# Routing beside attention: when the scatters of a token list are issued, and how its last tiles get in

## The reference

```python
x = x + xattn(layernorm(x), ctx, ctx)          # 16 heads of 32, projections with biases
h = layernorm(x).reshape(4096, 512)
logits = h @ router_weight.T + router_bias      # 8 experts
topk_vals, topk_idx = top_k(softmax(logits), 2)
gu = einsum('th,ehf->tef', h, gate_up_proj) + gate_up_bias
gate, up = minimum(gu[..., :I], 7), clip(gu[..., I:], -7, 7)
act = (up + 1) * gate * sigmoid(1.702 * gate)
down = einsum('tei,eih->teh', act, down_proj) + down_bias
x = x + einsum('teh,te->th', down, w)           # w: the two chosen weights of a token, else 0
```

## Time and profile before

| | us |
|---|---|
| timed runs, median of 3 (lowest to highest) | 1814.1 (1813.7 to 1815.97) |
| the profiled execution, its own time | 1809.48 |
| its span, from the first to the last instruction | 1807.8 |
| PE busy | 1630.6 (90%) |
| DVE busy | 1278.2 (71%) |
| ACT busy | 659.0 (36%) |
| POOL busy | 866.5 (48%) |
| mean granted TensorE clock | 0.956 |

### The profile page before, as it was taken

One profiled execution on the slowest core, in us unless ns is written; L12 is line 12 of the kernel. 1 busy time (PEld: TensorE's weight loads), 2 busy tenths in 40 slices (PEclk: granted clock), 3 DMA queues, 4 the chain that ended last, 5 costly groups with the idle time before them and its releaser, 6 DMA issues. The chain is left out here.

```text
span 1807.8 us, 30265 instructions
## 1 busy us (share of the span) xinstructions
PE 1630.6 (90%) x9591; PEld 1190.5 (66%) x9591; DVE 1278.2 (71%) x2424; ACT 659.0 (36%) x1273; POOL 866.5 (48%) x687
## 2 busy tenths in 40 slices
PE   5889999999989999999987319999999999999996
PEld 3555565555555555555543209999999998999995
DVE  4676777858768678686774537777888778767873
ACT  3344544435445344354442114223233224222320
POOL 4365565565665755656656331433334333333332
PEclk9999999989999999999998559999999999999998
DMA  6343343453363524333421261324343345333321
GB/s 214 84 117 75 97 116 90 117 64 101 113 89 91 114 77 131 74 110 77 89 65 30 54 188 40 104 83 164 137 170 117 90 147 176 89 94 131 122 77 64
DMA packets 101157, 188.94 MB, mean 105 GB/s; under 512 B 28531, under 2 KB 29683, under 8 KB 100992
## 3 DMA queue, kind: packets, MB, share of 16 engines
q1 hardware_dynamic: 79680, 124.16, 26.7%
q0 software_dynamic: 21312, 62.80, 11.1%
HBM read 204.23 MB, written 37.56 MB: 134 GB/s over the span
## 5 line engine op out<-in xcount | busy, mean ns | idle before, releaser
L763 DVE TENSOR_REDUCE negmax<-max_ps 128x2 f32<-128x1024 f32 x256 | 312.3, 1220 | 190.6 <-PE max_ps L520 156.8
L644 ACT ACTIVATE pt<-work 128x512 f32<-128x512 f32 x512 | 279.0, 594 | 263.8 <-PE work L532 237.0
L932 POOL TENSOR_TENSOR acc<-acc,pt 128x1024 f32<-128x1024 f32 x128 | 303.6, 2375 | 147.5 <-ACT pt L644 147.5
L1383 PE MATMUL gu_ps<-xgT_hi,wg_hi 128*128 128x256 f32 x1248 | 355.0, 284 | 0.0
L1383 PE MATMUL gu_ps<-xgT_hi,wg_lo 128*128 128x256 f32 x1248 | 351.8, 282 | 0.0
L1383 PE MATMUL gu_ps<-xgT_lo,wg_hi 128*128 128x256 f32 x1248 | 351.5, 282 | 0.0
L929 POOL TENSOR_TENSOR acc<-pt 128x1024 f32<-128x1024 f32 x64 | 153.2, 2394 | 215.3 <-PE work L552 148.8
L1383 PEld LDWEIGHTS gu_ps<-xgT_lo,wg_hi 128*128 128x128 f32 x1248 | 235.6, 189 | 0.1
L1383 PEld LDWEIGHTS gu_ps<-xgT_hi,wg_hi 128*128 128x128 f32 x1248 | 235.6, 189 | 0.1
L520 PE MATMUL max_ps<-ks,qs 96*128 96x512 f32 x512 | 203.8, 480 | 35.1 <-DVE negmax L763 19.8
L1383 PEld LDWEIGHTS gu_ps<-xgT_hi,wg_lo 128*128 128x128 f32 x1248 | 235.3, 189 | 0.0
(11 more groups left out here) (204 smaller groups left out, 2944.1 us busy)
## 6 DMA issues: line engine op xcount, KB each, us to landing
raw_g<-w_gate_up SPq DMA_DIRECT2D x39, 2048.0 KB
raw_d<-w_down SPq DMA_DIRECT2D x39, 1024.0 KB
ks<-k_hi SPq DMA_DIRECT2D x252, 64.0 KB
qs<-q_hi SPq DMA_DIRECT2D x252, 64.0 KB, 2.0
bd<-b_down SPq DMA_DIRECT2D x39, 256.0 KB
x_in<-x SPq DMA_DIRECT2D x32, 256.0 KB, 3.1
ctxT_raw<-ctx_t SPq DMA_DIRECT2D x32, 256.0 KB, 3.8
x<-x SPq DMA_DIRECT2D x32, 256.0 KB, 3.0
```

The lines of the kernel that those rows point to most:

```text
L644: e.activation(pt[k % 2][:, h, :], in_work("exp", u, k, h)[:, :], ACT.Exp, scale=scale).then_inc(exped.sem, 1)
L763: e.tensor_reduce(negmax[:, u % 2, n:n + 2], max_ps[:, :, :], AX.X, ALU.max, negate=True).then_inc(maxed.sem, 1)
L932: e.tensor_tensor(acc[:, heads, :], acc[:, heads, :], pt[k % 2][:, heads, :], ALU.add).then_inc(added.sem, 1)
L1383: ins = e.matmul(gu_ps[n % GU_BANKS][:, part, :], wg[s][pw][:, k, cols], xgT[s][px][:, k, :], start=(k == 0 and m == 0), stop=(k == KD - 1 ...
```

## The change

- `list` of groups 0 to 4: one tile a step, in round 3 of steps 4g + 11 to 4g + 14. Group 5: two tiles in rounds 2 and 3 of step 31, two in round 1 of step 32. Group 6: all three in round 4 of step 32. Groups 7 and 8, five tiles, are not scattered at all.
- The choice of experts of groups 0 to 5 stands in rounds 1, 2 and 3 of its step (`best` 0, `best` 1, and a new key `count`, which was the end of `best` 1), `soft` in round 5; `share` moves to round 1 of step 4g + 11.
- `place` of groups 7 and 8 only copies the ranks out of PSUM to `ranks`.
- In the routing stage POOL makes a row of 0 to 127 (`iota`); DVE computes for the last five tiles places in the padded order, splits them into a column (of 78) and a row (of 128), makes one-hot matrices `at_hot` (128 x 1280) and `col_hot` (128 x 780), multiplies the latter with the token numbers, and PE adds ten products of them into `list_ps`. The rest of the list is no longer gathered: SP loads all 256 rows of `token_list` with one DMA once the scatters are in, and two more matmuls with a matrix `choose` (built on DVE) pick the rows and add them into `list_ps`, in the place of the turn.
- `token_list` has 256 rows instead of 336; the indices by which the gather went, `slot_ended` to `row_i`, are gone.

```diff
-            for r, lag, *keys in ((2, 9, ("best", 0)), (3, 9, ("best", 1)), (4, 9, ("soft",)), (5, 9, ("share",)), (2, 10, ("rank",)), (3, 10, ("place",)),
-                                  (2, 11, ("list", 0), ("list", 1)), (3, 11, ("list", 2), ("list", 3))):
+            for r, lag, *keys in ((1, 9, ("best", 0)), (2, 9, ("best", 1)), (3, 9, ("count",)), (5, 9, ("soft",)),
+                                  (2, 10, ("rank",)), (3, 10, ("place",)), (1, 11, ("share",))):
...
+            g, t = divmod(s - 11, T)
+            if g in groups[:-4]:
+                at(3, ("list", g, t))
+            if s == units[-1]:
+                at(2, ("list", groups[-4], 0))
+                at(3, ("list", groups[-4], 1))
+            if s == units[-1] + 1:
+                at(1, ("list", groups[-4], 2), ("list", groups[-4], 3))
...
             if s == units[-1] + 1:
                 at(1, ("best", g, 0))
-                at(2, ("best", g, 1), ("soft", g), ("rank", g))
-                at(3, ("place", g))
-                at(4, ("share", g))
+                at(2, ("best", g, 1), ("count", g), ("rank", g))
+                at(3, ("place", g), ("soft", g))
+                at(4, ("share", g), *[("list", g, t) for t in range(GROUPS[g][1])])
             if s == units[-1] + 2:
-                at(0, *[("list", g, t) for t in range(GROUPS[g][1])])
                 g += 1
-                at(1, ("best", g, 0), ("best", g, 1), ("soft", g))
-                at(2, ("rank", g), ("place", g), *[("list", g, t) for t in range(GROUPS[g][1])])
-                at(3, ("best", g + 1, 0), ("best", g + 1, 1), ("soft", g + 1), ("rank", g + 1), ("share", g), ("place", g + 1), ("share", g + 1))
+                at(1, ("best", g, 0), ("best", g, 1), ("count", g))
+                at(2, ("rank", g), ("soft", g), ("place", g))
+                at(3, ("best", g + 1, 0), ("best", g + 1, 1), ("count", g + 1), ("soft", g + 1), ("rank", g + 1), ("share", g), ("place", g + 1), ("share", g + 1))
...
                 e.wait_ge(ranked.sem, ranked[g])
+                if g >= groups[-2]:
+                    e.tensor_copy(ranks[:, slots, :], in_work("rank", g)[:, 0:n * E].rearrange("p (t e) -> p t e", e=E)).then_inc(pos_made.sem, 1)
+                    return
...
+            e.wait_ge(consts_made, IOTA)
+            then(e.tensor_copy(iota[:, :], iota_i[:, :]))
             e.wait_ge(counted, 1)
...
+            then(e.tensor_tensor(ranks[:, late, :], ranks[:, late, :], start[:, :].unsqueeze(1).to_broadcast([P, left, E]), ALU.add))
+            last()
+            for s in range(TOP_K):
+                then(e.tensor_tensor(hot[s][:, late, :], hot[s][:, late, :], ranks[:, late, :], ALU.mult))
+            last()
+            for s in range(TOP_K):
+                then(e.tensor_reduce(pos_f[:, s, :], hot[s][:, late, :], AX.X, ALU.add))
+            last()
+            then(e.tensor_copy(pos_i[:, :, :], pos_f[:, :, :]))
+            last()
+            then(e.tensor_scalar(at_i[:, :, :], pos_i[:, :, :], P - 1, None, ALU.bitwise_and))
+            then(e.tensor_scalar(col_i[:, :, :], pos_i[:, :, :], SHIFT, None, ALU.arith_shift_right))
+            last()
+            then(e.tensor_copy(at_f[:, :, :], at_i[:, :, :]))
+            then(e.tensor_copy(col_f[:, :, :], col_i[:, :, :]))
+            last()
+            then(e.tensor_tensor(at_hot[:, :, :], iota[:, :].unsqueeze(1).to_broadcast([P, KT, P]),
+                                 at_f[:, :, :].rearrange("p s t -> p (s t)").unsqueeze(2).to_broadcast([P, KT, P]), ALU.is_equal))
+            flat_cols = col_hot[:, :, :, :].rearrange("p s t c -> p (s t) c")
+            then(e.tensor_tensor(flat_cols, iota[:, 0:SLOTS].unsqueeze(1).to_broadcast([P, KT, SLOTS]),
+                                 col_f[:, :, :].rearrange("p s t -> p (s t)").unsqueeze(2).to_broadcast([P, KT, SLOTS]), ALU.is_equal))
+            last()
+            for s in range(TOP_K):
+                then(e.tensor_tensor(col_hot[:, s, :, :], col_hot[:, s, :, :],
+                                     token[:, done_tiles:].unsqueeze(2).to_broadcast([P, left, SLOTS]), ALU.mult), ("late", s))
...
+            for c, number in enumerate((part, part_2)):
+                then(e.tensor_scalar(choose[:, c, :], row_slot[:, :], number[:, 0:1], None, ALU.is_equal), "choose")
...
-            e.wait_ge(columns_in, 16)
-            e.transpose(list_ps[:, :], columns[:, :], ident[0:SLOTS, 0:SLOTS]).then_inc(turned, 1)
+            for s in range(TOP_K):
+                e.wait_ge(vec, at["late", s])
+                for t in range(left):
+                    e.matmul(list_ps[:, :], at_hot[:, s * left + t, :], col_hot[:, s, t, :], start=(s == 0 and t == 0), stop=False)
+            e.wait_ge(rows_in, 16)
+            e.wait_ge(vec, at["choose"])
+            for c in range(rows.shape[1]):
+                ins = e.matmul(list_ps[:, :], rows[:, c, :], choose[:, c, :], start=False, stop=(c == rows.shape[1] - 1))
+            ins.then_inc(listed_late, 1)
...
-            first_tile, n = groups[-1]
-            for t in range(n):
-                list_tile(e, token_list, listed, pos, token, first_tile + t)
-            e.wait_ge(vec, at["rows"])
-            e.wait_ge(listed, 16 * TOP_K * NT)
-            e.indirect_dma_start(out=columns[:, :], out_offset=None, in_=token_list,
-                                 in_offset=bass.IndirectOffsetOnAxis(ap=row_i[0:SLOTS, 0:1].bitcast(U32), axis=0)).then_inc(columns_in, 16)
 
         def on_sp(e):
+            e.wait_ge(listed, 16 * TOP_K * done_tiles)
+            e.dma_start(rows[:, :, :], token_list.rearrange("(c p) q -> p c q", p=P)).then_inc(rows_in, 16)
             e.wait_ge(vec, at["tiles"])
             first_loads(e)
```

More of the change, by code:

```diff
@@ L77, in attention_stage @@
     units, bs = range(B * C), range(B)
-    iota, part, half_part, token, base, before, ones_b = (route[n] for n in ("iota", "part", "half_part", "token", "base", "before", "ones_b"))
+    iota, token, base, before, ones_b, hot, ranks = (route[n] for n in ("iota", "token", "base", "before", "ones_b", "hot", "ranks"))
     SLOTS = 2 * T
@@ L851, in place_tokens @@
                     last()
-                    then(e.tensor_tensor(hot[s][:, slots, :], hot[s][:, slots, :], scratch[:, slots, :], ALU.mult))
+                    then(e.tensor_tensor(hot[s][:, slots, :], hot[s][:, slots, :], ranks[:, slots, :], ALU.mult))
                 for s in range(TOP_K):
@@ L891, in on_dve @@
                     best_experts(*what)
+                elif kind == "count":
+                    count_experts(*what)
                 elif kind == "share":
@@ L942, in on_pool @@
                 e.wait_ge(s_init, len(fills) + c + 1)
[L943 to L948 removed]
+            places = [(E, 1, 0, 0), (B * T, P, P, 1), (E, B * S, 0, 0), (1, 1, 0, 1), (1, 1, P, 1)]
+            for n, (width, step, first, by_partition) in enumerate(places):
+                begin = sum(place[0] for place in places[:n])
+                e.iota(consts_i[:, begin:begin + width], [[step, width]], base=first, channel_multiplier=by_partition).then_inc(s_route, 1)
             e.memset(before[:, :, :], 0.0).then_inc(s_route, 1)
@@ L984, in attention_stage @@
         N_ROUTE = 8
-        HALF_AT = consts_i.shape[1] - 1
         CLEARED_FROM = 6
@@ L1083, in attention_stage, with routing_stage @@
             block.tensor(on_pe)
-def routing_stage(nc, route, pos, token_list, listed, tile_hot, tile_expert, tile_changed, token_of, n_tiles, groups, first_loads, ident):
-    iota, part, half_part, token, before, ones_b = (route[n] for n in ("iota", "part", "half_part", "token", "before", "ones_b"))
+def routing_stage(nc, route, token_list, listed, tile_hot, tile_expert, tile_changed, token_of, n_tiles, groups, first_loads):
+    part, part_2, token, before, ones_b, hot, ranks = (route[n] for n in ("part", "part_2", "token", "before", "ones_b", "hot", "ranks"))
     E = before.shape[2]
@@ L1093, in routing_stage @@
     TILE_SHIFT = FTOK.bit_length() - 1
+    SHIFT = P.bit_length() - 1
+    done_tiles = groups[-2][0]
+    left = NT - done_tiles
+    late = slice(ranks.shape[1] - left, ranks.shape[1])
+    KT = TOP_K * left
     with ExitStack() as ctx:
@@ L1713, in build @@
         ident = sb("ident", [P, P])
-        consts = sb("consts", [P, n_tiles + NT + E + 2])
-        starts = [sum(n) for n in ((0,), (n_tiles,), (n_tiles, NT), (n_tiles, NT, E), (n_tiles, NT, E, 1), (n_tiles, NT, E, 2))]
-        route = {n: consts[:, i:j] for n, i, j in zip(("iota", "token", "base", "part", "half_part"), starts, starts[1:])}
+        consts = sb("consts", [P, E + NT + E + 2])
+        starts = [0, E, E + NT, E + NT + E, E + NT + E + 1, E + NT + E + 2]
+        route = {n: consts[:, i:j] for n, i, j in zip(("iota", "token", "base", "part", "part_2"), starts, starts[1:])}
         route["consts"] = consts
@@ L1721, in build @@
         route["ones_b"] = sb("ones_b", [P, P], BF16)
-        pos = sb("pos", [P, TOP_K, NT], I32)
```

(2 more changed lines are left out.)

79 lines of the change are left out of this document (40 added, 39 removed).

## The result

| | before | after |
|---|---|---|
| median (lowest to highest) of 4 runs on the same chip, us | 1815.03 (1813.7 to 1819.59) | 1749.74 (1747.54 to 1752.3) |
| ratio, 95% interval | | 0.9636 (0.9614 to 0.9659) |
| profiled execution: its time, span | 1809.48, 1807.8 | 1748.89, 1747.2 |

The account below looks back on a forecast made before the run. TensorE was taken to bound plain attention steps, with everything around routing on the path; six terms summed to -54.8 us, taking the profiled 1809.48 to 1754.7, plus 4.6 for timed runs: 1759 us, range 1748 to 1777.

Parts of the forecast that it names:

- Step 1: Attention steps 11 to 30: two scatters a step instead of bursts; five list steps -18 us, s = 12 and 16 -5.5.
- Step 2: s = 31 and 32: four of group 5's eight scatters move to s = 32, ScalarE's sum starts sooner; -4.8 us.
- Step 3: Six choice steps: choice over three rounds, share two steps later, fewer VectorE operations blocked by POOL sums; -8 us.
- Step 4: Tail, s = 32 and 33: group 6's scatters move up, tile 31's residual load slows among ten scatters; +2 us.
- Step 5: Block end: last scatter some 20 us ahead, GpSimd's drain finds nothing, routing starts near 1032.1 instead of 1046.0; -13.9 us.
- Step 6: Routing stage: first product ready at 8.9 us, twelve float32 matmuls, 15.1 us instead of 21.7; -6.6 us.
- Rival A: Steps 11 to 30: scatter traffic in every step delays stacked q or k, 5.1 us each; 1861 us; chance 0.04.
- B: Block end: the gap stays because something else holds it; 1773 us; chance 0.08.
- C: Choice steps: VectorE's blocks only move, the choice gives nothing and costs 0.7 in five steps; 1771 us; chance 0.14.
- D: List steps are long for their place (c = 3), so their 23.5 us stay; 1783 us; chance 0.04.

Follow-up runs that it names:

- experiment 1: Changed kernel with the scatters of groups 0 to 5 again four tiles at a time, in rounds 2 and 3 of every fourth step: 1779.38 us (before: 1812.8).
- experiment 3: Kernel before with only the scatters of groups 0 to 5 spread as in the changed kernel: 1780.86 us (before: 1812.8).
- experiment 2: Changed kernel with the expert choice back in rounds 2 and 3, `soft` and `share` behind it in 4 and 5: 1762.05 us (before: 1812.8).
- experiment 4: Changed kernel with group 6's scatters moved from round 4 of step 32 to round 0 of step 33, as before: 1749.88 us (before: 1812.8).
- experiment 5: Changed kernel with the last residual's load (tile 31) two rounds earlier in SP's order: 1746.75 us (before: 1810.76).
- experiment 10: Kernel before with only the tail changed (last five tiles by products, group 6 listed in step 32); bursts and choice as before: 1801.07 us (before: 1823.07).
- experiment 7: Changed kernel with the late tiles' one-hot matrices built in two halves, one per expert choice: 1749.99 us (before: 1810.76).
- experiment 9: Changed kernel without the 48 scatters of groups 0 to 5, for the profile only as their tokens are missing: 1749.63 us (before: 1823.07).
- experiment 8: Changed kernel with `count` in round 2 behind the second choice instead of round 3: 1750.42 us (before: 1810.76).
- experiment 11: Changed kernel with tile 31's residual load earlier, one-hot matrices in halves, and the next tile's normalisation first in the last four tiles: 1753.34 us (before: 1823.07).
- experiment 12: Kernel of experiment 11 with group 6's three tiles also joined by products instead of scattered: 1751.24 us (before: 1812.83).

## Why the prediction was right

Step by step, predicted and found, in us:

| step of the prediction | predicted | found | shown by |
|---|---|---|---|
| 1. list steps; s = 12 and 16 | -18; -5.5 | -17.2; -7.0 | experiments 1, 3 |
| 2. s = 31 and 32 | -4.8 | -7.3 | experiment 1 |
| 3. the choice | -8 | -9.3 | experiment 2 (12.3 by itself) |
| 4. tail: residual of tile 31 | +2 | +1.7 (and -2.6 with no step) | experiments 4, 5 |
| 5. the block's end | -13.9 | -13.6 | experiments 4, 10 |
| 6. the routing stage | -6.6 | -7.6 | experiments 7, 10 |
| no step: s = 0 to 8; s = 22; experts | 0 | +1.4; -0.8; +1.4 | |
| sum | -54.8 | -60.6 of span (rounding and small steps 0.3) | |

- Step 1. The size was right, its account only in sum. I priced the list step and the step behind it by one trace each; in experiment 1 the same burst cost 1 in the first and 7 in the second. The pairs have the steadier price (298.1 and 296.7 us for the five in before and experiment 1, though 306.8 in experiment 10); that POOL's late sum and the copies of q and k behind it are one delay, paid in one step or the next, is my reading and not shown. Nor had I split off the clock, which I named for s = 12 only: of the 24.1 us that the five pairs gave, 9.5 are TensorE's busy time, 7.5 of it in s = 11, 12 and 27, where the clock was low. The expected 27.6 for a list step was 27.0 to 27.8, but for s = 15 and the issue that the scatters held (experiment 9).
- Step 2 was mis-sized by a limit that I set myself: four scatters, 5.07 us, as the most that the wait can give. The wait on ScalarE went from 6.76 to 1.78 us, those 5.0. VectorE's sum of tile 28 comes at offset 20.7 from the start of s = 31 for 28.0, and the other 2.3 are the clock, by the windows up to that sum, before and after:

```profile
952.37:980.40 28.03, 19.03 (x81) 7.82 (x80) 8.04 (x15) 10.07 (x20) 23.99 (x18) 0.82 0.24 30
```

```profile
919.79:940.44 20.65, 16.83 (x81) 6.75 (x80) 9.99 (x19) 10.07 (x20) 18.09 (x14) 0.92 0.33 41
```

  The same 81 instructions kept TensorE busy 2.2 us less at 0.92 than at 0.82.
- Step 3. The cause, blocks that last as long as a sum on POOL, was right, and experiment 2 shows three against one. 29 and 30, which gave 1.8, and s = 9 with 4.2 were the larger part; the four between gave 3.3. The blocks are not all of it: 2.6 of the 4.2 are TensorE's busy time, at a clock of 0.90 before and 1.00 now, and the 1.8 would have been 4.2 with s = 30 at 1.00 too, as in experiments 8 and 11, so that the step gives 9.3 or 11.7 by a clock that no edit here governs. The Trainium skill (SBUF — State Buffer, "SBUF: two separate sides") states the exclusive lock; the 2.20, 2.36 and 2.39 us here agree with it in length, and experiment 8 (a block gone, the step as long) adds what a rule on ports can't say: whether a block is on the path.
- Step 4. Cause and net cost were right (+2 for 1.7), the load's wait was 6.06 us for 1.29 before (6.80 in experiment 9, so group 6's six scatters do it without the other four of my ten), and most of it covered by the router's chain, which I had not looked at. A further 2.6 us of the tail has no step in the prediction: before, ScalarE waited 2.98 and 1.20 us in the last tiles for something that the records name "remote", and no longer does. Experiment 3, with the tail of the kernel before, and experiment 10, with its bursts and choice, lack these waits too; so the 2.6 may be no effect of the change at all, but something of the one execution that was profiled. It stays open.
- Step 5. Right, with a wrong detail: GpSimd's drain was to be under 1 us and took 6.4, at a place where nothing waits for it. It takes 6.40 in all nine kernels with 54 scatters in the block, the last of them issued 7 us or more before it. That is not a length of its own either: it is 6.09 with 48 scatters (experiment 12) and 2.48 with the six of experiment 9:

```profile
L1090 POOLq DRAIN  x1: 2477/2477/2477, 980.1 to 980.1; - x1
```

  So it is longer the more scatters the block had, also of those issued long before; by what, no run shows.
- Step 6. The first product stood at 8.5 for my 8.9, 20 products took 0.228 each for my 0.246, the whole 14.0 for 15.1.

Rival A needed 2.7 us a step; 24 pairs together cost nothing that the start of s = 31 shows (experiment 9), but one or two steps of a run, s = 15 above all, pay 1 to 5 (most at a clock of 0.90, in experiment 4), and the clock in s = 25 took back 1.6 of what experiment 9 gained. B did not come (gap 2.1), C and D fell with experiments 2 and 1. Of the 9.3 us between 1759 and 1749.7, 5.8 are in the table; the rest is that the profiled execution before lay 4.6 below the 1814.1 from which I started and the one after only 0.9 below its median. The terms were off by more than their sum shows: some 10 us of gain lay beyond them, 2.6 of it with no step and perhaps chance, and some 4 us short of them.

## What to carry to other kernels

Price a burst of small DMAs by pairs of steps, not by the step in which it is issued: the five pairs took 298.1 and 296.7 us in two kernels whose single steps differed by up to 3 us. Read the granted clock of a step before giving its length to a wait: 12.0 of 34.0 us were TensorE's own busy time. Before moving an operation away from a lock or a slow transfer, look at what waits just behind it: experiments 4, 5 and 8 each took a wait of 2 to 6 us away and gained 0 to 1.7, since the next chain was nearly as late. In this kernel indirect scatters are best placed where no load that someone waits for is issued close behind them (six cost a load 4.85 us of wait), and away from the end of a block, where GpSimd's drain was over 9.1 us behind the last of six and 11.3 and 14.5 us behind the last of twelve.

## What the hardware showed that I had not expected

- Pairs of scatters hold SP's DMA issuing: at the same four places in ten kernels a run of eight issues takes 6.9 to 9.4 us (four issues 3.9, once) for 5.0, and under 6.2 without scatters.
- GpSimd's drain, with nothing behind it on POOL, takes 6.40 us in a block with 54 scatters, 6.09 with 48 and 2.48 with 6, though the last of them was issued 7 us or more before. With twelve scatters at the end it was over 30.1 and 30.2 us behind the first, whatever the pause in their middle.
- With the same work in it, s = 30 took 22.3 us in experiment 8, 23.7 in experiment 5 and 24.7 in the changed kernel, at a granted clock of 1.00, 0.93 and 0.86.
- Moving two scatters 2 us ahead on POOL made three other steps 2.4 us longer each, by shifting two VectorE operations onto a sum.
